# Second moments of x2 accumulated at the end of the attention block, with PSUM held by both blocks

## What is computed

```python
x = x + xattn(layernorm(x), ctx_1024, ...)      # x2 is this sum
def ffn(x, ...):                                # x is layernorm(x2)
    q = einsum("bnd,de->bne", x, w_q)           # 2048 query columns
    mean, var = mean(q, (0, 1)), var(q, (0, 1)) # over all 4096 tokens
    q = (q - mean) * rsqrt(var + 1e-5) * gamma + beta
    # scores against 128 keys per half, top 8 of each half, top 8 of the 64 pairs,
    # 64 rows of down_embed and up_embed gathered for each token, gelu, weighted sum
return x + ffn(layernorm(x), ...)
```

## Time and profile before

| what | us |
|---|---|
| median of 3 runs | 3657.74 |
| lowest and highest run | 3656.67, 3663.62 |
| the profiled execution, whole | 3661.88 |
| its span, first to last instruction | 3660.1 |
| attention ends, norm starts | 496 |
| norm ends, first product of the expert block | 573.88 |
| first gather is issued | 640 |

### The profile page before, as it was taken

How to read it: one execution, slowest core, us unless ns; L and a number is a source line. 1 busy time by engine, 2 the same in 40 slices (tenths; PEclk the granted TensorE clock), 3 DMA queues, 4 the chain that set the end, 5 groups by cost and what they waited for, 6 DMA issues and landing times.

```text
span 3660.1 us, 33789 instructions
## 1 busy us (share of the span) xinstructions
PE 3004.9 (82%) x8870; PEld 1498.1 (41%) x8870; DVE 2441.3 (67%) x5247; ACT 1723.2 (47%) x5110; POOL 2063.2 (56%) x2193
## 2 busy tenths in 40 slices
PE   7999999688888878787777787878788878778877
PEld 6787756333333333333333333333333333333333
DVE  5777735466766767676666666767666667666774
ACT  1222201455555545455555554555455555555554
POOL 1111131466666666666666666666666666666664
PEclk9999999899999999899999998999998999999888
DMA  5111100799999999999999999999999999999997
GB/s 190 52 60 57 52 17 24 264 362 371 363 364 373 368 370 357 360 369 367 369 368 365 363 367 375 361 371 361 369 380 362 363 371 371 368 371 362 363 364 293
DMA packets 324681, 1132.55 MB, mean 309 GB/s; under 512 B 36187, under 2 KB 36827, under 8 KB 323880
## 3 DMA queue, kind: packets, MB, share of 16 engines
q0 software_dynamic: 294912, 1073.87, 76.8%
q1 hardware_dynamic: 28800, 55.92, 4.4%
q10 hardware_dynamic: 808, 0.99, 0.1%
HBM read 1113.87 MB, written 16.78 MB: 309 GB/s over the span
## 4 chain that ended last, share of the span: by engine, by line
PE 23%; DVE 18%; ACT 15%; another core or an unknown queue 15%; issue 13%; DVEq 0%; ACTq 0%
PE expert_out_ps L1378 16%; ACT rows L1213 10%; DVE rows L1030 6%; PE expert_score_ps L1357 5%; DVE expert_diag L1044 3%; DVE expert_top_s L945 2%; DVE expert_top_i L953 2%; ACT expert_act_h L1225 2%; ACT expert_more_rows L1213 1%; PE expert_out_ps L1292 1%; DVE expert_best_i L976 1%; DVE expert_coef L1036 1%; ACT L1225 1%; DVE expert_more_rows L1030 1%
## 5 line engine op out<-in xcount | busy, mean ns | idle before, releaser
L865 POOL DMA_INDIRECT rows<-in_table,expert_idx x1824 | 1726.8, 947 | 973.7 <-issue 590.1
L1378 PE MATMUL expert_out_ps<-rows,expert_diag 128*128 128x512 f32 x3648 | 1757.4, 631 | 504.8 <-DVE expert_diag L1044 275.5
L1213 ACT ACTIVATE rows<-rows 128x512 f32<-128x512 f32 x1824 | 1123.7, 617 | 818.8 <-DVE expert_coef L1036 452.7
L1378 PEld LDWEIGHTS expert_out_ps<-rows,expert_diag 128*128 128x128 f32 x3648 | 722.1, 202 | 1490.1 <-issue 1047.3
L1030 DVE TENSOR_TENSOR rows<-rows,expert_xn_ps 128x2048 f32<-128x2048 f32 x456 | 1038.4, 2277 | 10.6 <-issue 5.8
L1036 DVE TENSOR_TENSOR expert_coef<-expert_act_h,expert_prob 128x4 f32<-128x4 f32 x512 | 81.5, 159 | 866.6 <-remote 500.8
L1357 PE MATMUL expert_score_ps<-amat,expert_xnT 128*128 128x512 f32 x992 | 466.9, 594 | 3.8 <-ACT expert_score_ps L1204 3.1
L1044 DVE TENSOR_TENSOR expert_diag<-expert_bias_ps,expert_coef 128x512 f32<-128x512 f32 x512 | 347.9, 679 | 13.9 <-issue 11.2
L1213 ACT ACTIVATION_READ_ACCUMULATOR rows<-rows 128x1 f32 x1824 | 340.4, 187 | 0.0
L1378 PE MATMUL expert_out_ps<-expert_more_rows,expert_diag 128*128 128x512 f32 x448 | 218.0, 632 | 85.8 <-DVE expert_diag L1044 38.3
L1357 PEld LDWEIGHTS expert_score_ps<-amat,expert_xnT 128*128 128x128 f32 x992 | 188.3, 190 | 243.9 <-issue 237.1
(11 more groups left out here) (135 smaller groups left out, 2178.4 us busy)
## 6 DMA issues: line engine op xcount, KB each, us to landing
rows<-in_table,expert_idx POOLq DMA_INDIRECT x1824
x_t<-in_x SPq DMA_DIRECT2D x32, 256.0 KB, 2.9
attention_xr_t<-in_x SPq DMA_DIRECT2D x32, 256.0 KB, 2.7
x_dram<-rows SPq DMA_DIRECT2D x32, 256.0 KB, 2.0
expert_x_t<-x_dram SPq DMA_DIRECT2D x32, 256.0 KB
out_y<-expert_x_t SPq DMA_DIRECT2D x32, 256.0 KB
rows<-in_w_q SPq DMA_DIRECT2D x4, 1024.0 KB, 6.9
rows<-in_w_qT SPq DMA_DIRECT2D x4, 1024.0 KB, 9.3
```

The source lines that it names most:

```text
L865: pool.indirect_dma_start(four(n)[:, k, :], None, table[:, :], bass.IndirectOffsetOnAxis(ap=idx[:, t % 2, at:at + 1], axis=0))\
L1213: ins = act.activation(down, down, ACT.Copy, accum_out=hid[:, j % RING, k:k + 1])
L1378: mm = pe.matmul(out_ps[:, par, :], diag[:, j % RING, k, :], four(t * HALVES + j)[:, k, D:2 * D], start=(j == 0 and k == 0), stop=(j == HA ...
```

## The change

The norm block is gone. Its parts stand elsewhere:

- Pool normalizes x2 in place, one tile in each attention step (`norm_x2`, tile s-4), once the tile's copy has gone to DRAM, and adds it to xsum. Pool's steps are no longer in loops.
- The tensor engine's products for the second moments read these tiles. Eight tiles are placed in the drain of the attention pipeline, four in step 32 and four in step 33, 23 follow behind step 34, then the product that makes the mean row, then the last tile. No tile is placed in steps 0 to 31.
- All eight banks of PSUM are one tensor, `banks`, which both blocks use. The sums of the second moments lie in banks 0 to 3, which held scores and queries until step 31. They are copied out at the start of the expert block, by ACT (j = 0 and 3, and the mean row) and DVE (j = 1 and 2), scaled and doubled in the same instruction. The first products of the expert block wait for these copies, each for its own.
- The mean is no longer subtracted from the matrix. Instead the square of each query's mean is subtracted from its variance, four queries at a time.
- `cov` lies in the last 512 columns of each part of `amat`, the mean row, xsum and the constant in `bias_row`.

```diff
-        with ExitStack() as own:
-            norm_block(nc, maker(own, "norm_"), x2_all, mean_var2, rstd2, cov, mu_row)
...
+                if -4 in has:
+                    norm_x2(s - 4, par, half - 2)
+
+            def norm_x2(t, par, half):
+
+                x2 = x2_all[:, bass.ts(t, D)]
+                wait(pool, "rstd2_done", t + 1)
+                wait(pool, "mean_var2_kept", t + 1)
+                pool.wait_ge(x2_out[par], (half + 1) * 16)
+                pool.tensor_scalar(x2, x2, mean_var2[:, bass.ds(t, 1), 0:1].rearrange("p a b -> p (a b)"),
+                                   rstd2[:, bass.ds(t, 1)], ALU.subtract, ALU.mult)\
+                    .then_inc(ev["xn2_done"], 1)
+                wait(pool, "xn2_done", t + 1)
+                wait(pool, "xsum_done", t)
+                pool.tensor_tensor(xsum, xsum, x2, ALU.add).then_inc(ev["xsum_done"], 1)
+
+            pool.memset(xsum, 0.0)
+            pool.memset(inv_tokens, 1.0 / (NT * P)).then_inc(ev["sums_ready"], 1)
+            wait(pool, "sums_ready", 1)
             first_rstd(0, 0)
-            pipeline(pool, step)
+            straight(range(NT + 4), step)
...
+            def second_moments(tiles, first=False):
+
+                if first:
+                    wait(pe, "masked", NT)
+                    wait(pe, "qT_done", NT)
+                for _ in range(tiles):
+                    t = moments_left.pop(0)
+                    wait(pe, "xn2_done", t + 1)
+                    x2 = x2_all[:, bass.ts(t, D)]
+                    for j in range(KC):
+                        pe.matmul(banks[:, j, j * P:D], x2[:, j * P:(j + 1) * P], x2[:, j * P:D],
+                                  start=(t == 0), stop=(t == NT - 1))
...
+                if draining and s < NT + 2:
+                    second_moments(2, first=(s == NT))
                 if back2:
                     turn_attention(s - 2)
+                if draining and s < NT + 2:
+                    second_moments(2)
...
             pipeline(pe, step)
+            second_moments(len(moments_left) - 1)
+            wait(pe, "x2_done", NT)
             wait(pe, "xsum_done", NT)
+            pe.matmul(att_ps, inv_tokens, xsum, start=True, stop=True)
+            second_moments(1)
...
+            def keep_moments(j):
+
+                own, beside = slice(j * P, (j + 1) * P), slice((j + 1) * P, D)
+                dve.tensor_scalar(cov[:, j, own], banks[:, j, own], 1.0 / (NT * P), None, ALU.mult)
+                dve.tensor_scalar(cov[:, j, beside], banks[:, j, beside], 2.0 / (NT * P), None, ALU.mult)\
+                   .then_inc(ev["cov_kept"], 1)
...
-                    if m % 4 == 3:
-                        dve.tensor_scalar(var[:, m - 3:m + 1], var[:, m - 3:m + 1], BN_EPS, None,
-                                          ALU.add).then_inc(ev["var_eps"], 1)
                     dve.tensor_tensor_reduce(junk, mu_row, wq2T[:, m, :], 1.0, 0.0,
                                              ALU.mult, ALU.add, mean_q[:, m:m + 1])\
                        .then_inc(ev["mean_done"], 1)
+                    if m % 4 == 3:
+                        some = slice(m - 3, m + 1)
+                        wait(dve, "mean_done", m + 1)
+                        dve.tensor_tensor(scale[:, some], mean_q[:, some], mean_q[:, some], ALU.mult)\
+                           .then_inc(ev["squared"], 1)
+                        wait(dve, "squared", m // 4 + 1)
+                        dve.scalar_tensor_tensor(out=var[:, some], in0=var[:, some], scalar=BN_EPS,
+                                                 in1=scale[:, some], op0=ALU.add, op1=ALU.subtract)\
+                           .then_inc(ev["var_eps"], 1)
...
+            keep_moments(0)
+            keep_moments(3)
+            act.activation(mu_row, banks[:, 7, :], ACT.Copy).then_inc(ev["mu_kept"], 1)
             turned(0, 0)
```

156 lines of the change are left out of this document (48 added, 108 removed).

## The result

| | before | after |
|---|---|---|
| median | 3656.67 us (7 runs, 3654.88 to 3663.62) | 3640.36 us (7 runs, 3638.38 to 3649.38) |
| profiled execution | 3661.88 | 3638.82 (span 3637.0) |
| first product of the expert block | 573.88 | 561.82 |
| DVE's second variance of the query moments | 581.21 | 566.41 |
| first gather issued | 639.98 | 625.18 |

The changed kernel takes 0.9956 of the time, interval 0.9944 to 0.9968. That is 16.3 us less, by the interval 11.7 to 20.5. The forecast was 15.5 us less, 3642.

A forecast was written before the change was run, and what follows sets the result against it. PE was taken to bound attention and the chain behind it, gathers the expert block. Drain 8.7, hand-over 4.0 and query clock 2.8 sum to 15.5 us: median 3657.7 to 3642.2, range 3634 to 3650.

The forecast's parts named there:

- What bounds the kernel: PE bounds attention and the chain from 467 to 640 us; gathers pace the expert block, so starting them earlier ends earlier.
- The moments stay PE's work: Second moments: all 32 tiles still cost PE 68.8 us, eight in the drain, 24 behind it, none beside full attention steps.
- rival D: Attention: the 32 tiles of moments find free time on PE, 77 us go, 3581 us; chance 0.01.
- Drain idles, clock and mean row: Attention drain to last tile: 7.45 us of idles filled, 2.1 for the clock, 0.87 lost to the mean row: 8.7 us.
- Hand-over: Last tile to first query product: 5.63 us become 1.58, gaining 4.0 us, between 2.6 and 4.4.
- The term for the copies: Before the first query product: ACT's two copies of block row 0 out of PSUM take 0.38 + 0.57 us.
- Clock at the queries: First query products: the low clock after the idle goes, gaining 2.8 us, or nothing at the other end.
- Rival A: First query products: the clock falls all the same and 2.8 us are not gained; 12.7 us gain, 3645 us; chance 0.15.
- Pool: Attention steps: Pool's added tensor_scalar and sum, 2.6 us a step, are hidden in 10.80 us idle, even at three times the price.
- Rival C: Attention: Pool's new work holds DVE's query scaling; slower from 0.62 us, 3676 us if held a whole operation; chance 0.05.
- Rival B: Before the seventh gather group: the 9.20 us stall changes; hole closes, 3637 (chance 0.15), or grows, 3647 us (0.10).
- rival E: Filled idles return as other waits, or gathers hide half the shift: gain under 7.3 us, 3652 us; chance 0.06.

The follow-up runs named there:

- e6: Changed kernel with one of the four tiles of moments placed ahead of the values product in steps 32 and 33, first series: 3670.59 us.
- e11: Changed kernel with one of the four tiles of moments placed ahead of the values product in steps 32 and 33, third series: 3318.09 us, 0.9947 of before.
- again: The changed kernel unaltered, run once more in the first series beside the kernel before: 3670.68 us, 0.996 of before.
- again_2: The changed kernel unaltered, run once more in the third series beside the kernel before: 3319.82 us, 17.1 us less than before.
- e3: Changed kernel with two more 128x512 tensor_scalar on Pool in each step, result unread: 3331.47 us, 0.9987 of before.
- e4: Changed kernel with four more 128x512 tensor_scalar on Pool in each step, result unread: 3332.66 us, 0.9993 of before.
- e5: Changed kernel with six more 128x512 tensor_scalar on Pool in each step, result unread: 3447.71 us, 1.0329 of before.
- e7: Changed kernel with five more copies of the mean row by ACT ahead of its copies of the moments: 3324.66 us, 0.9968 of before.
- e9: Changed kernel with the x2 normalization moved from Pool to DVE, Pool keeping the sum: 3321.53 us, 0.9953 of before.
- e8: Changed kernel with the first gather held back until amat is complete: 3332.20 us, 3.7 us below before.
- e1: Changed kernel without moments in the drain, all but the last tile behind step 34: 3676.98 us, 0.997 of before.
- e2: Kernel before, norm block and drain kept, with only the changed copying out of the sums and mean subtraction from the variance: 3680.47 us, 0.9984 of before.

## Why the prediction was right, point by point

**What bounds the kernel.** Right. The positions add up: `out` came 0.7 earlier (469.49 to 468.80), the stretch to the second variance became 14.1 shorter (111.72 to 97.61), and nothing changed from there to the first gather (58.77 both times). The 0.7 belong to no term: `e6` and `e11` are one kernel and have `out` at 469.98 and 468.78. Without them and the low clock of one execution, `again` gives the cleaner sum: 564.63 - 468.68 = 95.95, and 111.72 - 95.95 = 15.8 less from `out` to the second variance, against 15.5. From Pool's first gather to its last it took 2652.2 to 2653.1 us in `again_2`, `e3`, `e4`, `e5`, `e7`, `e9` and `e11`, although the first came anywhere from 621.66 to 752.43; so what moves the first gather moves the last. With `e5` and `e8`, a later first gather came out at the end, each against its own before, as 114 of 116 us and as 13 of 15.

**The moments stay PE's work, rival D.** Right: by their modelled lengths 71.0 us of them in both profiles and 69.4 in `e1`, where they stand in one piece at full clock; none beside a full step.

**Drain idles, clock and mean row: 8.7 us.** In the profiled run 7.0: from `out` to the end of the last tile's issue 568.25 - 469.49 = 98.76 before, 560.57 - 468.80 = 91.77 after. In both repetitions it was 8.7, since the low clock of 1.7 us was missing there. `e1` gave 3.4 for the four short waits, 3.2 by the forecast. The clock's share was some 1.8 instead of 2.1, since a tile at full clock takes (557.56 - 507.92) / 23 = 2.158 and not 2.149. The statement that the clock would be 1.00 throughout was wrong for one of three profiles of this kernel.

**Hand-over: 4.0 us.** 5.63 - 1.25 = 4.4. The term for the copies was too long: the second overlaps the first (561.20 to 561.68), and the product follows 0.14 behind.

**Clock at the queries: 2.8 us.** (4.77 + 2.56) - (2.59 + 2.00) = 2.7. This was the least certain term, with an idle of 1.6 between rows of 1.35 and 3.8. The new idle of 1.1 kept the clock, and `e7` shows that 4.2 in the same place loses it. Rival A did not happen; between 1.1 and 4.2 nothing was measured at this place.

**Pool.** Hidden, as said, but the size was wrong. The tensor_scalar takes 2.08 to 2.35 us, above my upper bound of 1.27, which I had taken from the two-input operation of the same size; the 0.44 of the prediction's other estimate is about a fifth of it. The new work is 3.5 us a step and not 2.6. It fits all the same: the changed kernel has 8.0 us of idle a step left on Pool, and even two more fit. "Even at three times the price" was wrong: it counted the idle alone, and `e3`, at 7.7 us of new work a step nearly at that price, lost 0.35 a step with idle left on Pool. The Trainium skill ("GPSIMD Engine Reference", "4.1 Engine selection") calls one input roughly line rate and two inputs about half; here the operation with one input and two scalars per partition was the slower of the two, 2.1 to 1.27, and DVE's 0.54 is a quarter of it. Of the choice of engine, `e9` shows that DVE does the same work in a quarter of the time, and that it makes no difference to this kernel that can be told.

**Rival C.** Its mechanism exists, its place was right to be cleared: the query scaling stayed at 0.69. I had looked at that one instruction, and `norm_x` behind it was held for 0.16 us on average. Its slack hid that. Its condition, DVE waiting for an operation of Pool, came true to 0.94 of the sum's 1.27 us in `e3`. The next instruction that Pool's sum can meet, the subtraction, has less.

**Rival B.** Neither half happened: 9.20 became 9.19. Nor did rival E: no new wait on PE took the place of those filled.

**From the first gather to the end.** 14.8 us by position, 16.3 by the medians, 23.1 by the two profiled executions. The rest of 1.5 is inside the interval; the other 6.8 of the profiled pair lie in the gather stage, where single runs of one kernel spread by 9 us before and by 11 after; no cause of the change was looked for there.

**The range.** Its ends do not follow from the words beside them: 3637 less 0.4 for a short hand-over is 3636.6 and not 3634, and 3645 with 1.4 for a long one and 5 for the hole is 3651.4 and not 3650. The measured 3640.36 lies inside either way.

## What to carry to other kernels

Sum a gain from positions in one chain up to the stage that sets the pace, and hold it against positions later; the medians of this kernel, with intervals of 4 us to either side, could not tell terms of 2 us apart. When work moves to an idle engine, its own idle time is not the only limit: look at what the neighbour sharing its memory runs at that moment, above all pairs of operations with two inputs in SBUF, and which of the two begins first. Placing independent work in front of each dependent one in a drain paid for the waits (3.4 us, `e1`); the clock was 1.00 around those short waits before, and its gain (1.8 and 2.7) came with the two idles of about 4 us that the change took away.

## What was not expected of the hardware

- Pool's tensor_scalar of 128x512 float32 with a subtract and a multiply took 2.08 us, and up to 2.35 where DVE's `norm_x` began early in it, more than its sum of two such tiles (1.27).
- A sum on Pool stopped DVE's subtraction in SBUF for 0.94 of 1.08 us in which they overlapped, and was itself not longer; a tensor_scalar on Pool in its place did nothing to it. Where the subtraction began first, the sum took 2.43 instead. The tensor_scalar on Pool did hold DVE's tensor_scalar of the same size, 0.91 for 0.54.
- After the same wait of 1.34 us in the same place the clock was 0.83 over ten microseconds in one execution and 1.00 in the two repetitions, as in `e4`, `e7`, `e8` and `e9` behind 1.34 and in `e1`, `e2` and the kernel before behind 1.35. Behind the 1.69 of `e3` it was 0.83, behind the 1.91 of `e5` 1.00. The length of the wait alone does not decide it.
- The chips differ by 10% on the same kernel, 3336 to 3688 us, and the changed kernel's first gather comes within 2 us on three of them (623.40 to 625.18), so that the difference lies behind it. The stretch below, of `again_2`, stands beside the last line of the first block above: 412 GB/s and not 367, with PE's clock at 0.99 and not 0.91. The wait of 9.2 us ahead of the seventh group is absent there too. Its cause on the slower ones, ACT standing still for 10.99 and 7.28 us under the first gathers with no releaser in its queue's trace, stays open.

```profile
1400.00:2100.00 700.00, 607.88 (x1372) 254.91 (x1370) 539.71 (x1180) 413.09 (x1271) 508.89 (x538) 0.99 1.03 412
```

```profile
650.81 0.60 ACT L1230 ACTIVATE amat<-banks 128x512 f32<-128x512 f32 x1 [10.99 <-issue]
...
659.26 0.60 ACT L1230 ACTIVATE amat<-banks 128x512 f32<-128x512 f32 x1 [7.28 <-remote]
```
